# Linear attention on one core: the gamma product, the clip and the value scale change engines

## The reference, cut to what matters

```python
kh = _split_heads(_layernorm(k @ wk, ln_gamma, ln_beta))
vh = _split_heads(_layernorm(v @ wv, ln_gamma, ln_beta))
k_prime = (jax.nn.relu(kh) + EPS_K) * em          # EPS_K = 1e-06
vh = vh * em
kv = jnp.einsum('bhnd,bhne->bhde', k_prime, vh)
z = 1.0 / (jnp.einsum('bhnd,bhd->bhn', q_prime, k_prime.sum(axis=-2)) + EPS_K)
att = jnp.einsum('bhnd,bhde,bhn->bhne', q_prime, kv, z)
```

## Time and profile before

| | |
|---|---|
| median of 3 runs | 891.3 us (888.0, 891.3, 892.58) |
| profiled execution | span 888.3 us from first to last instruction (its device time as a whole is not listed apart) |
| VectorE, TensorE busy | 590.6 us (66%), 715.8 us (81%) |
| ScalarE, GpSimd busy | 482.0 us (54%), 251.1 us (28%) |
| L905, L902 (GpSimd, 48 each) | 64.2 us, 61.1 us |
| L1023, L1034, L1038, L1044 (VectorE, 48 each) | 57.9, 33.2, 32.6, 27.9 us |
| L1051 (VectorE, 16) | 15.1 us |

### The profile page before, as it was taken

One profiled execution on the slowest core, in us unless ns is written; L12 is line 12 of the kernel. 1 busy time (PEld: TensorE's weight loads), 2 busy tenths in 40 slices (PEclk: granted clock), 3 DMA queues, 4 the chain that ended last, 5 costly groups with the idle time before them and its releaser, 6 DMA issues.

```text
span 888.3 us, 19613 instructions
## 1 busy us (share of the span) xinstructions
PE 715.8 (81%) x7277; PEld 492.1 (55%) x7277; DVE 590.6 (66%) x1145; ACT 482.0 (54%) x718; POOL 251.1 (28%) x236
## 2 busy tenths in 40 slices
PE   1588888876436478986799999999999997699998
PEld 1466666665222225653565566666566664457776
DVE  7699999996678676754567676668677675421111
ACT  1366666663225316664567766767666675463332
POOL 7177777774100540220122102222202210000000
PEclk9899999997565759997999999999999999889999
DMA  3122222141770074894959898899998977011101
GB/s 121 35 70 70 69 69 69 69 147 35 58 87 1 0 118 74 103 126 68 106 92 126 116 127 118 122 125 123 122 139 101 126 80 113 10 48 47 47 26 33
DMA packets 59459, 74.16 MB, mean 83 GB/s; under 512 B 35308, under 2 KB 40166, under 8 KB 59422
## 3 DMA queue, kind: packets, MB, share of 16 engines
q1 hardware_dynamic: 59422, 73.65, 52.9%
HBM read 32.61 MB, written 1.40 MB: 38 GB/s over the span
## 4 chain that ended last, share of the span: by engine, by line
PE 48%; DVE 30%; issue 11%; DMA 5%; SPq 3%; ACT 3%; DVEq 1%; POOL 0%; ACTq 0%
PE ps L601 7%; PE ps L492 7%; DVE ss L1023 6%; PE ps L588 6%; PE ps L659 6%; PE ps L671 6%; DVE mx L1222 6%; PE ps L484 5%; PE ps L478 5%; DMA QS<-QD 3%; DVE arena L1038 3%; DVE arena L1044 2%; DVE xn L977 2%; PE ps L513 2%; DVE wv L1034 1%
## 5 line engine op out<-in xcount | busy, mean ns | idle before, releaser
L1222 DVE TENSOR_REDUCE mx<-ps 128x1 f32<-128x500 f32 x336 | 215.0, 674 | 115.4 <-PE ps L492 113.9
L825 ACT ACTIVATE P<-ps,kbias,kscale 125x896 f32<-125x896 f32 x192 | 210.4, 1097 | 97.3 <-PE ps L588 93.0
L918 POOL TENSOR_TENSOR KP<-kvall,KP 128x1500 bf16<-128x1500 f32 x16 | 48.5, 3031 | 344.8 <-ACT KP L781 344.8
L492 PE MATMUL ps<-KP,Qb 128*128 128x500 bf16 x336 | 135.3, 404 | 9.7 <-issue 4.4
L601 PE MATMUL ps<-P,Vp 125*32 125x112 f32 x3072 | 116.4, 269 | 3.1 <-issue 1.7
L427 PE MATMUL ps<-wkv,cT 128*125 128x256 f32 x384 | 91.9, 383 | 0.8 <-ACT arena L744 0.8
L601 PEld LDWEIGHTS ps<-P,Vp 125*32 125x32 f32 x3072 | 68.6, 110 | 42.9 <-issue 36.0
L441 PE MATMUL ps<-arena 125*128 125x130 f32 x384 | 57.6, 294 | 37.3 <-DVE arena L1044 34.5
L744 ACT ACTIVATE arena<-ps,wv 125x128 f32<-125x128 f32 x192 | 54.8, 368 | 58.0 <-DVE arena L1038 58.0
L441 PEld LDWEIGHTS ps<-arena 125*128 125x128 f32 x384 | 48.2, 196 | 56.1 <-DVE arena L1044 52.8
L588 PE MATMUL ps<-QS,arena 128*128 128x112 bf16 x768 | 67.5, 215 | 12.5 <-issue 6.1
(11 more groups left out here) (189 smaller groups left out, 1038.8 us busy)
## 6 DMA issues: line engine op xcount, KB each, us to landing
cT<-ctxT_dram SPq DMA_DIRECT2D x32, 750.0 KB, 4.4
KS<-KP SPq DMA_DIRECT2D x48, 375.0 KB, 12.9
arena<-KP SPq DMA_DIRECT2D x48, 375.0 KB, 12.9
QS<-QD SPq DMA_DIRECT2D x96, 28.0 KB, 15.9
wgu<-w_dram SPq DMA_DIRECT2D x8, 256.0 KB, 2.8
silu<-w_dram SPq DMA_DIRECT2D x8, 256.0 KB, 2.6
x<-xh_dram SPq DMA_DIRECT2D x1, 512.0 KB, 3.3
mixed<-att SPq DMA_DIRECT2D x16, 28.0 KB
```

The source lines that it names most:

```text
L492: ins = nc.tensor.matmul(ps[:, bank, 0:KCW], q[:, 128 * c:128 * c + 128], KP[par][0][:, KCW * k:KCW * k + KCW], start=True, stop=True)
L825: nc.scalar.activation(P[t % 2][0:TK, :].rearrange("p (k n) -> p k n", k=2), src, ACT.Exp, scale=kscale[0:TK, bass.ds(n, 1)], bias=kbias[0 ...
L1222: ins = v.tensor_reduce(mx[:, c, k:k + 1], ps[:, bank, 0:KCW], AX.X, ALU.max)
```

## The change

GpSimd no longer multiplies by gamma. VectorE's key product becomes four `scalar_tensor_tensor` instructions, one a tile: keys from PSUM, times the reciprocal (a scalar for each partition), times gamma. VectorE loses the value scale and `relu`; GpSimd gets both, the value scale ahead of its wait for the keys, the clip behind the beta addition, in the same group. ScalarE's `values` waits for `wv_ready` too, and VectorE's reciprocal waits for `wv_ready` of the group two before, since it overwrites what GpSimd reads. In `state`, L1051 becomes a tensor_tensor with the PSUM column broadcast. The line numbers after it differ by a few: L1029 is the norm reduction, L1038 the reciprocal, L1043 the key products, L904 the value scale, L908 the beta addition, L912 the clip.

```diff
 def values(n, k):                                  # ScalarE
     act.wait_ge(sem("kn_ready"), n + 1)
+    act.wait_ge(sem("wv_ready"), n + 1)
     act.wait_ge(sem("kv_done"), n + 1)
...
 nc.gpsimd.tensor_copy(VN[0:TK, k, :, D:D + 2], ...).then_inc(sem("emc_ready"), 1)
+pool.wait_ge(sem("rk_ready"), n + 1)
+if not (first and k < 2):
+    pool.wait_ge(sem("vn_ready"), n - 1)
+nc.gpsimd.tensor_tensor(wv[0:TK, k % 2, :], rk[0:TK, k % 2, :, 1],
+                        em2[0:TK, bass.ds(b * T + GT * g, GT)], ALU.mult).then_inc(sem("wv_ready"), 1)
 pool.wait_ge(sem("kn_ready"), n + 1)
 kn = KN[0:TK, k, :, :]
-nc.gpsimd.tensor_tensor(kn, kn, bc(row[0:TK, GAMMA, :], 1, [TK, GT, D]), ALU.mult).then_inc(sem("kg_ready"), 1)
-pool.wait_ge(sem("kg_ready"), n + 1)
 nc.gpsimd.tensor_tensor(kn, kn, bc(row[0:TK, BETA, :], 1, [TK, GT, D]), ALU.add).then_inc(sem("kb0_ready"), 1)
+pool.wait_ge(sem("em_ready"), 1)
+pool.wait_ge(sem("kb0_ready"), n + 1)
+nc.gpsimd.tensor_scalar(kn, kn, 0.0, EPS_IN, ALU.max, ALU.add).then_inc(sem("kp_ready"), 1)
...
 def keys(b, n, k, first_pair):                     # VectorE
     dve.wait_ge(sem("sdk_ready"), n + 1)
+    if not (first_pair and k < 2):
+        dve.wait_ge(sem("wv_ready"), n - 1)
     v.reciprocal(r.rearrange("p t j -> p (t j)"), sdk[0:TK, k % 2, :]).then_inc(sem("rk_ready"), 1)
     dve.wait_ge(sem("rk_ready"), n + 1)
-    if not (first_pair and k < 2):
-        dve.wait_ge(sem("vn_ready"), n - 1)
-    v.tensor_tensor(wv[0:TK, k % 2, :], r[:, :, 1], em2[0:TK, bass.ds(b * T + GT * g, GT)], ALU.mult)
     dve.wait_ge(sem("kv_done"), n + 1)
-    v.tensor_tensor(KN[0:TK, k, :, :], y, bc(r[:, :, 0], 2, [TK, GT, D]), ALU.mult).then_inc(sem("kn_ready"), 1)
+    for t in range(GT):
+        c0 = 1024 * g + 256 * t
+        ins = v.scalar_tensor_tensor(KN[0:TK, k, t, :], ps2[0:TK, c0:c0 + D], r[:, t, 0:1],
+                                     row[0:TK, GAMMA, :], ALU.mult, ALU.mult)
+    ins.then_inc(sem("kn_ready"), 1)
-def relu(n, k):
-    dve.wait_ge(sem("kb0_ready"), n + 1)
-    kn = KN[0:TK, k, :, :]
-    v.tensor_scalar(kn, kn, 0.0, EPS_IN, ALU.max, ALU.add).then_inc(sem("kp_ready"), 1)
...
-    v.tensor_scalar(kvall[:, bass.ds(b, 1), D:KVW], hmask[:].unsqueeze(1), kv[:, D + 1:D + 2], None, ALU.mult)
+    v.tensor_tensor(kvall[:, bass.ds(b, 1), D:KVW], hmask[:].unsqueeze(1),
+                    kv[:, D + 1:D + 2].unsqueeze(1).broadcast_to([128, 1, H]), ALU.mult)
```

More of the change, by code:

```diff
@@ L899, in keys @@
                                       emcat[0:TK, bass.ds(b * T + GT * g, GT), :]).then_inc(sem("emc_ready"), 1)
+                pool.wait_ge(sem("rk_ready"), n + 1)
[3 more added lines that the diff above has]
+                                        em2[0:TK, bass.ds(b * T + GT * g, GT)], ALU.mult).then_inc(sem("wv_ready"), 1)
                 pool.wait_ge(sem("kn_ready"), n + 1)
                 kn = KN[0:TK, k, :, :]
-                nc.gpsimd.tensor_tensor(kn, kn, bc(row[0:TK, GAMMA, :], 1, [TK, GT, D]),
-                                        ALU.mult).then_inc(sem("kg_ready"), 1)
-                pool.wait_ge(sem("kg_ready"), n + 1)
                 nc.gpsimd.tensor_tensor(kn, kn, bc(row[0:TK, BETA, :], 1, [TK, GT, D]),
                                         ALU.add).then_inc(sem("kb0_ready"), 1)
+                pool.wait_ge(sem("em_ready"), 1)
+                pool.wait_ge(sem("kb0_ready"), n + 1)
+                nc.gpsimd.tensor_scalar(kn, kn, 0.0, EPS_IN, ALU.max, ALU.add).then_inc(sem("kp_ready"), 1)
             def pair(i):
@@ L1031, in keys @@
                 dve.wait_ge(sem("rk_ready"), n + 1)
-                if not (first_pair and k < 2):
-                    dve.wait_ge(sem("vn_ready"), n - 1)
-                v.tensor_tensor(wv[0:TK, k % 2, :], r[:, :, 1], em2[0:TK, bass.ds(b * T + GT * g, GT)],
-                                ALU.mult)
                 dve.wait_ge(sem("kv_done"), n + 1)
-                y = ps2[0:TK, 1024 * g:1024 * g + 1024].rearrange("p (t n) -> p t n", t=GT)[:, :, 0:D]
-                v.tensor_tensor(KN[0:TK, k, :, :], y, bc(r[:, :, 0], 2, [TK, GT, D]),
-                                ALU.mult).then_inc(sem("kn_ready"), 1)
-            def relu(n, k):
-                dve.wait_ge(sem("kb0_ready"), n + 1)
-                kn = KN[0:TK, k, :, :]
-                v.tensor_scalar(kn, kn, 0.0, EPS_IN, ALU.max, ALU.add).then_inc(sem("kp_ready"), 1)
+                for t in range(GT):
[3 more added lines that the diff above has]
+                ins.then_inc(sem("kn_ready"), 1)
             def state(b, par):
@@ L1050, in state @@
                 v.tensor_tensor(kvtmp[:, par, :], kv[:, 0:D], gmask[:], ALU.mult).then_inc(sem("kvt_ready"), 1)
-                v.tensor_scalar(kvall[:, bass.ds(b, 1), D:KVW], hmask[:].unsqueeze(1), kv[:, D + 1:D + 2], None,
-                                ALU.mult)
+                v.tensor_tensor(kvall[:, bass.ds(b, 1), D:KVW], hmask[:].unsqueeze(1),
+                                kv[:, D + 1:D + 2].unsqueeze(1).broadcast_to([128, 1, H]), ALU.mult)
                 dve.wait_ge(sem("kvt_ready"), b + 1)
@@ L1063, in pair @@
                         norms(n, k)
-                        if not (first and k < 2):
-                            relu(n - 2, (k - 2) % SLOTS)
                         if g == 0 and not first:
@@ L1070, in _ @@
             in_pairs(dve, pair, B // 2)
-            last = NG * B - 1
-            relu(last - 1, SLOTS - 2)
-            relu(last, SLOTS - 1)
             state(B - 2, 0)
```

## The result

The changed kernel takes 898.9 us (median of 6, 895.0 to 900.6) against 890.95 for the kernel before (median of 6): ratio 1.0086, 95% interval 1.0059 to 1.0114. It is slower, by more than half a per cent. The profiled execution has a span of 893.2 and a time of 895.0, the shortest of the six.

A forecast was written before the change was run, and what follows sets the result against it. Bound taken: two GpSimd products in series with the key product. Savings of 16.2 (33 plain groups), 7.0 (14 state groups) and 0.9 (end), less 0.4 (first group), make 23.7: 891.3 to 867.6 us, range 857 to 884.

The forecast's parts named there:

- The ring of two GpSimd products and the key product: Linear attention's key and value stage, plain groups: these in series, with the held value scale, set the 3.39 us period.
- VectorE's turn 2.87: VectorE in a plain group: 1.58 from reduction to reciprocal, 0.24 to the key products, 1.05 for those four.
- ScalarE's ring 2.86: Plain group, us: key product's end, 0.03, four values 1.13, square root and handover 0.33, 0.24, key product 1.13.
- The clip on GpSimd: 125x512 clip in GpSimd's turn: taken as 0.95 us, between a memset-based 0.61 and the addition's 1.34; turn 2.82.
- The scale in time for the values, kv matmuls not late: GpSimd reaches the next scale at 2.82, values need it at 2.90; kv matmuls, ready at 3.0, lose nothing.
- the prediction's own sign for it: The ring is wrong if ScalarE's L745 is released by GpSimd rather than by VectorE.
- The state groups, 3.60: Groups with `state`: 4.10 falls to 3.60 us, taking 0.7 over a plain group, the middle of 0.2 and 1.2.
- Rival 1: GpSimd mildly the pace: clip costs 1.34 like the add, plain-group turn 3.13, time 874; chance 0.13.
- Rival 2: Slower: shared port holds the new key products behind GpSimd's clip; 899, or 917 with the longer ring; chance 0.06.
- Rival 3: Slower: GpSimd's clip takes two passes, 2.6 us, making its turn 4.4 and the time 931; chance 0.03.
- Rival 4: No gain: a small delay in each hop brings the period back to 3.35, time 888; chance 0.05.
- the three rings: Plain-group cycles of VectorE (2.87), ScalarE (2.86) and TensorE (2.89 at most), within 0.03 us; period taken as 2.90.

The follow-up runs named there:

- the two runs that each cut it in one place: On the kernel before: only the value scale moved to GpSimd, 874.4 us, ratio 0.983; only gamma moved to VectorE, 872.9 us, ratio 0.981.
- times-and-plus kernel: Changed kernel with GpSimd's clip replaced by times 1.0 plus 1e-6, without the maximum: 864.9 us, ratio 0.970 to the kernel before.
- half-clip kernel: Changed kernel with GpSimd's clip over two of the four tiles, the others left unclipped: 859.5 us, ratio 0.967 to the kernel before.

## Why the prediction was right or wrong, point by point

The forecast was 867.6 and faster; the result is slower, and outside the range.

- *What bounds the kernel before*: right. The ring of two GpSimd products and the key product, closed by the held value scale, is shown by the two runs that each cut it in one place (0.983, 0.981).
- *Four products for one, 1.05 where 0.60 was; VectorE's turn 2.87; ScalarE's ring 2.86*: right, 2.86 in the kernel without a clip.
- *GpSimd's small instructions at 0.19, the addition at 1.34*: right. They start 0.15 apart, the addition takes 1.27 with 0.16 behind it, and all of the turn beside the clip is 3.71 - 1.92 = 1.79; the prediction's terms for it give 1.34 + 0.07 + 0.19 + 0.19 = 1.79.
- **The clip on GpSimd, "the middle, 0.95" between 0.61 and 1.34** (the middle is 0.98, which changes nothing): this is the step that failed. It takes 1.92. GpSimd's turn is then 3.71 and not 2.82, and all else follows. The upper bound was not a bound. I took the addition for one since it has the same elements and one input more; but a row bounds an instruction from above only if it does the same kind of operation, and no row on GpSimd had a maximum. With the kind of operation that the rows did have, multiply and add, the true price is 0.62, at the lower bound.
- *The page weighed there*: The Trainium skill, page GPSIMD Engine Reference, section Elementwise — side-by-side cycle accounting, gives 1.8 cycles an element as the best case, an estimate of 0.77 us here. The measured 0.62 for multiply and add is below that, and the measurement decides. The 1.92 of the clip is far above it, which a best case does not exclude; it is also 4.7 times the 0.41 that the same clip takes on VectorE when nothing holds it.
- *The scale in time for the values, kv matmuls not late*: the kv matmuls are hardly late: they start at 109.67, when the clip (to 109.62) and the y matmuls (to 109.65) have both just ended. The scale is, which follows from the clip, and the prediction's own sign for it came: ScalarE's L745 starts 0.08 after GpSimd's scale ends. It was late only because the whole queue was; moving it ahead of the clip gave 0.07 a group.
- *The state groups, 3.60*: right in kind (L1055 is held), and hidden here behind GpSimd. Where the clip takes 0.62 the group with `state` costs 3.55. That this is so near 3.60 is in part luck: 3.60 was the middle of two cases around a clip of 0.95.
- *Rival 1* had a clip of 1.34. *Rival 2*, the port holding the key products, is wrong: 1.13 in every row. *Rival 3* is what happened in kind: GpSimd the pace by a dear clip, with "from a clip of 1.8 on the whole loses". It measured 1.92, and lost a little. Its reason, two passes for two operations, is not borne out: multiply and add are two as well and take 0.62. I put it at 2.6 and gave it 0.03, for want of a row that spoke for it; but there was no row against it either, and a size without any row of its kind deserved more. *Rival 4* is wrong: without the clip the three rings run at 2.86, with no delay in the hops.

## What to carry to other kernels

An instruction that moves to another engine has no bound from that engine's rows until one of them does the same kind of arithmetic: measure it alone, or give the dear case a real chance. When a busy engine seems the limit, look for tiny instructions with long durations; here a 125x4 product of 0.16 us recorded as 0.90 was the sign of a ring through another engine, and taking that one instruction out of it gave 1.7%. And count an engine's turn before giving it work: of the two pieces that GpSimd was given the value scale fit, and the clip cost more than the rest of the change had gained.

## What the runs showed of the hardware that I had not expected

- GpSimd's tensor_scalar on 125x512 float32: multiply and add 0.62 us; maximum alone 1.49; maximum and add 1.92; the last on 125x256 1.07. On VectorE maximum and add on 125x512 take 0.41 where nothing holds them. Two inputs with one addition take 1.27 on GpSimd.
- VectorE and GpSimd hold each other both ways: VectorE's clip waits for GpSimd's addition (0.59 instead of 0.41), and GpSimd's copy of eight elements waits for VectorE's clip (0.39 instead of 0.19). An instruction with PSUM, a pointer scalar and one SBUF tensor isn't held (1.13 for four, beside GpSimd in every group of the changed kernel). By the Trainium skill, SBUF — State Buffer, section Who interferes with whom, at most one SBUF input outside the two-port modes does not contend; the trace agrees, with the pointer not counted.
- A wait decided by a narrow margin: in the times-and-plus kernel the state's last instruction starts at 102.64 and GpSimd's L912 at 102.70, yet it is VectorE's that is held: it lasts 0.81, until 0.13 after L912's end. In the half-clip kernel the same pair starts 0.05 apart in the same order (102.14 and 102.19), and VectorE's lasts 0.59 and ends 0.52 before GpSimd's does. So there it did not wait for the whole of GpSimd's instruction. Both repeat in all 12 groups with `state` of the loop's body; what decides between them is open.
- The softmax part, in which nothing was changed, ran at a granted clock of 0.97 or 0.98 in five of fourteen profiles and at 1.00 in the others, and lasted 3 to 9 us longer in those five: as much as a whole stage's gain of the kind looked for here.
